# States turned to rows by VectorE blocks and a DRAM scratch instead of TensorE transposes, in a fused graph network and expert kernel

## What is computed

```
h = layernorm(x)
for l in 0, 1, 2:
    m    = h @ weight[l]
    aggr = A^T m                      # A = (adj != 0), per graph
    h    = GRU(aggr, h)               # r, z = sigmoid(...), n = tanh(i_n + r*h_n), h = (1-z)*n + z*h
x = x + h
H = gelu(layernorm(x) @ W1 + b1)      # 128 -> 512
probs = softmax(H @ Wg + bg)          # 8 experts; the best one is taken
x = x + probs[e] * (H @ Wd[e] + bd[e])
```

## Time and profile before

| what | value |
|---|---|
| time, median of 3 runs | 492.29 us (492.11 to 492.55) |
| profiled execution, first to last instruction | 490.1 us |
| around that span (median less span) | 2.2 us |
| mean granted TensorE clock | 0.997 of full speed (2.4 GHz) |
| busy, share of the span | TensorE 98%, VectorE 76%, GpSimd 77%, ScalarE 68% |
| graph network, gate, experts | about 12 to 285 us, to 365 us, to 490 us |

### The profile page before, as it was taken

One profiled execution on the slowest core, in us unless ns is written; L12 is line 12 of the kernel. 1 busy time (PEld: TensorE's weight loads), 2 busy tenths in 40 slices (PEclk: granted clock), 3 DMA queues, 4 the chain that ended last, 5 costly groups with the idle time before them and its releaser, 6 DMA issues.

```text
span 490.1 us, 10428 instructions
## 1 busy us (share of the span) xinstructions
PE 480.0 (98%) x3247; PEld 401.9 (82%) x3247; DVE 370.0 (76%) x1158; ACT 334.7 (68%) x595; POOL 376.1 (77%) x371
## 2 busy tenths in 40 slices
PE   8999999999999999999999999999999999999994
PEld 4788888888888888888888877777769999999994
DVE  4898678789887898888887798878977555655552
ACT  4886996667976768966787698988763554445531
POOL 5389986789988899979778656777777776377576
PEclk9999999999999999999999999999999999999998
DMA  8889000000000000000000000111353342233110
GB/s 217 234 242 289 0 1 0 1 1 1 1 1 2 0 1 2 0 3 0 1 0 1 0 2 18 59 62 57 110 136 100 119 124 86 71 97 90 33 48 24
DMA packets 37317, 27.38 MB, mean 56 GB/s; under 512 B 6140, under 2 KB 33920, under 8 KB 37264
## 3 DMA queue, kind: packets, MB, share of 16 engines
q1 hardware_dynamic: 31344, 17.40, 12.8%
q0 software_dynamic: 4320, 8.93, 5.2%
q10 hardware_dynamic: 1600, 0.40, 0.4%
HBM read 17.12 MB, written 10.04 MB: 55 GB/s over the span
## 4 chain that ended last, share of the span: by engine, by line
PE 94%; ACT 2%; DVE 2%; POOL 1%; issue 1%; POOLq 0%; DVEq 0%
PE bank L484 20%; PE bank L486 19%; PE bank L485 19%; PE bank L736 13%; PE bank L507 4%; PE bank L531 4%; PE bank L530 4%; PE bank L672 3%; PE bank L722 2%; PE bank L629 1%; PE bank L596 1%; PE bank L537 1%; ACT adj_i L948 1%; PE bank L564 1%; PE bank L569 0%
## 5 line engine op out<-in xcount | busy, mean ns | idle before, releaser
L948 ACT ACTIVATE adj_i<-bank,b1c 128x512 f32<-128x512 f32 (+1 forms) x136 | 91.3, 685 | 72.8 <-PE bank L486 72.3
L375 POOL TENSOR_TENSOR diff<-hT,n_sb 128x512 f32<-128x512 f32 x48 | 77.1, 1607 | 12.0 <-ACT n_sb L834 12.0
L451 POOL DMA_INDIRECT sorted_rows<-xrow,pos x64 | 62.2, 972 | 20.0 <-issue 17.9
L736 PE MATMUL bank<-wd_sb,adj_i 128*128 x568 | 66.7, 275 | 0.0
L377 POOL TENSOR_TENSOR diff<-z_sb,diff 128x512 f32<-128x512 f32 x48 | 63.5, 1323 | 3.8
L736 PEld LDWEIGHTS bank<-wd_sb,adj_i 128*128 128x128 f32 x568 | 65.1, 192 | 0.2
L484 PE MATMUL bank<-ag_hi,wf_hi 128*128 128x512 f32 x144 | 61.0, 424 | 0.0
L484 PE MATMUL bank<-hT_hi,w_hi 128*128 128x512 f32 (+1 forms) x136 | 58.3, 429 | 0.9 <-ACT adj_i L948 0.7
L486 PE MATMUL bank<-ag_hi,wf_lo 128*128 128x512 f32 x144 | 57.1, 397 | 0.0
L485 PE MATMUL bank<-ag_lo,wf_hi 128*128 128x512 f32 x144 | 56.7, 394 | 0.0
L484 PE MATMUL bank<-hT_hi,whh_hi 128*128 128x512 f32 x132 | 54.0, 409 | 0.0
(11 more groups left out here) (185 smaller groups left out, 1158.2 us busy)
## 6 DMA issues: line engine op xcount, KB each, us to landing
adj_i<-sorted_rows SPq DMA_DIRECT2D x71, 72.0 KB
xrow<-in_x_dram SPq DMA_DIRECT2D x16, 256.0 KB, 3.7
adj_i<-in_adj_dram SPq DMA_DIRECT2D x16, 256.0 KB, 4.0
sorted_rows<-xrow,pos POOLq DMA_INDIRECT x64, 2.3
sorted_rows<-padrow SPq DMA_DIRECT2D x9, 72.0 KB
out_dram<-cand,home POOLq DMA_INDIRECT x39
bd_bc<-in_L_ffn_bd_dram SPq DMA_DIRECT2D x1, 512.0 KB, 4.1
out_dram<-n_sb,home POOLq DMA_INDIRECT x32
```

The costliest lines, as they stand in the source:

```text
L375: nc.gpsimd.tensor_tensor(diff[:, b, :], hT[:, g, :], n_sb[:, b, :], ALU.subtract).then_inc(diff_ok, 1)
L451: nc.gpsimd.indirect_dma_start(out=sorted_rows, out_offset=bass.IndirectOffsetOnAxis(ap=pos[:, g, j:j + 1], axis=0), in_=xrow[:, g * GR + ...
L736: last = nc.tensor.matmul(o, HT[:, sg % 2, k, j * P:(j + 1) * P], wd_sb[:, bass.ds(at + k * P, P)], start=(k == 0), stop=(k == KC - 1))
L948: nc.scalar.activation(HT[:, hb, k, 0:n], HB[k][:, 0:n], ACT.Gelu, bias=b1c[:, k:k + 1]).then_inc(done, 1)
```

## The change

For states of layers 0 and 1 (32 of the 48 units) the transposes on TensorE go. VectorE transposes the 32x32 blocks of the state into a tile `blocks`; SyncE writes that to a DRAM scratch `swap` with one DMA of 256 KB, waits until it has landed, and reads it back with four DMAs of 64 KB each, which put the blocks in their places; the result `hn` has nodes on partitions with the four graphs interleaved. The sum over neighbours takes plain float32 operands, four products a unit in place of eight, from `xn` in layer 0 and `hn` in layers 1 and 2; `hn_hi`, `hn_lo` and all that makes them are removed on ScalarE, VectorE and GpSimd. The loads of groups 8 to 15 are issued after the first eight states are turned, the weights of the second half after sixteen.

```diff
+    SUB = 32
+    QP = P // SUB
+    swap = nc.dram_tensor("swap", (2, QP, P, P), fp32).ap()
-        A = sb("A", [P, QUAD, NT], f32r)
+        A = sb("A", [P, QUAD, NT])
-        hn_hi, hn_lo = sb("hn_hi", [P, 2, NT], f32r), sb("hn_lo", [P, 2, NT], f32r)
+        blocks = sb("blocks", [P, 2, NT])
+        hn = sb("hn", [P, 2, NT])
+        TURNED = [u for u in range(UN) if layer(u) < LAYERS - 1]
+        FIRST_LOADS = GROUPS // 2
...
# SyncE
+            def state_turned(k):
+                b = k % 2
+                sp.wait_ge(blk_ok, k + 1)
+                hold(sp, hn_in[b], k // 2 * QP * 16)
+                sp.dma_start(swap[b].rearrange("s p e -> p s e"),
+                             blocks[:, b, :].rearrange("p (s e) -> p s e", s=QP)).then_inc(blk_out, 16)
+                sp.wait_ge(blk_out, (k + 1) * 16)
+                if k >= 2:
+                    sp.wait_ge(ag_ps, made("all", TURNED[k - 2] + QUAD))
+                for f in range(QP):
+                    sp.dma_start(hn[:, b, f * P:(f + 1) * P], swap[b, :, f * SUB:(f + 1) * SUB, :]).then_inc(hn_in[b], 16)
+            for g in range(2, FIRST_LOADS):
+                load_group(g)
+            for k in range(2 * QUAD):
+                state_turned(k)
+            for g in range(FIRST_LOADS, GROUPS):
+                load_group(g)
+            for k in range(2 * QUAD, 4 * QUAD):
+                state_turned(k)
...
+            for k in range(4 * QUAD, len(TURNED)):
+                state_turned(k)
# GpSimd
-                if first(s + 1):
-                    first_rows_low(s + 1)
# TensorE
             def neighbours(u):
                 if layer(u) == 0:
                     hold(pe, adj_ok, made("first", u))
...
+                    rows_of = xn[:, u % QUAD, :].rearrange("p (g e) -> p g e", g=GR)
                 else:
-                    hold(pe, hnhi_ok, made("later", u))
-                    hold(pe, hnlo_ok, made("later", u))
+                    k = made("later", u) - 1
+                    pe.wait_ge(hn_in[k % 2], (k // 2 + 1) * QP * 16)
+                    rows_of = hn[:, k % 2, :].rearrange("p (c g) -> p g c", g=GR)
                 for j in range(GR):
...
-                    nc.tensor.matmul(pAG[:, c], hn_hi[:, u % 2, c], A[:, u % QUAD, c], start=True, stop=False)
-                    last = nc.tensor.matmul(pAG[:, c], hn_lo[:, u % 2, c], A[:, u % QUAD, c], start=False, stop=True)
+                    last = nc.tensor.matmul(pAG[:, c], rows_of[:, j], A[:, u % QUAD, c], start=True, stop=True)
...
-                if exists(u):
+                if first(u):
                     unit_turned(u)
# ScalarE: rows_high, the two halves in opening, and hn_hi in step_gnn removed
# VectorE: rows_low_half, rows_low_early, and hn_lo in step_gnn removed
+            def state_blocks(u):
+                k = made("inner", u) - 1
+                dve.wait_ge(h_ok, made("all", u))
+                hold(dve, blk_out, (k - 1) * 16)
+                nc.vector.transpose(blocks[:, k % 2, :].rearrange("p (s e g) -> p g s e", g=GR, s=QP),
+                                    hT[:, u % QUAD, :].rearrange("p (g s e) -> p g s e", g=GR, s=QP)).then_inc(blk_ok, 1)
...
                     state(s - 2)
+                    if layer(s - 2) < LAYERS - 1:
+                        state_blocks(s - 2)
```

More of the change, by code:

```diff
@@ L171, in build @@
             sem(n) for n in ("hh_ps", "r_ps", "z_ps", "in_ps", "ag_ps", "t_ps", "f_ps"))
[L172 to L175, removed]
+        aghi_ok, r_ok, z_ok, n_ok, hthi_ok, h0_ok, h0hi_ok = (
+            sem(n) for n in ("aghi_ok", "r_ok", "z_ok", "n_ok", "hthi_ok", "h0_ok", "h0hi_ok"))
+        aglo_ok, h_ok, h0lo_ok, rhn_ok, cand_ok, x1_ok, adj_ok = (
+            sem(n) for n in ("aglo_ok", "h_ok", "h0lo_ok", "rhn_ok", "cand_ok", "x1_ok", "adj_ok"))
+        blk_ok, blk_out, hn_in = sem("blk_ok"), sem("blk_out"), [sem("hn_in"), sem("hn_in_odd")]
         bn_ok, mv_ok, var_ok, rstd_ok, xn_ok, shift_ok = (
             sem(n) for n in ("bn_ok", "mv_ok", "var_ok", "rstd_ok", "xn_ok", "shift_ok"))
-        xn_half, x0hi_half = sem("xn_half"), sem("x0hi_half")
-        diff_ok, zd_ok, htlo_ok, x0lo_ok, x0lo_first = (
-            sem(n) for n in ("diff_ok", "zd_ok", "htlo_ok", "x0lo_ok", "x0lo_first"))
+        diff_ok, zd_ok, htlo_ok = (sem(n) for n in ("diff_ok", "zd_ok", "htlo_ok"))
         g_bn, g_mv, g_rstd, g_xn, g_t, g_xhi, g_xlo, g_w1, g_h, g_lg, g_lgT = (
@@ L239, in ahead @@
         def ahead(s):
-            return (3, 3, 2, 1, 3) if s < 3 else (9, 8, 5, 2, 2)
-        STATS, SCALE, NORMAL, SPLIT, EDGES = range(5)
+            return (3, 3, 2, 3) if s < 3 else (9, 8, 5, 2)
+        STATS, SCALE, NORMAL, EDGES = range(4)
         EARLY_STATS = GROUPS - QUAD
@@ L295, in _, with load_group @@
             load_adj(1)
-            for g in range(2, GROUPS):
+            def load_group(g):
                 sp.wait_ge(x_in[g % 2], g // 2 * 16)
@@ L365, in _ @@
             nc.gpsimd.memset(xrow[:, :, TOKEN + 1:ROW], 0.0).then_inc(g_tok, 1)
[L367 to L370, removed]
             def old_state(u):
@@ L498, in unit_turned @@
             def unit_turned(u):
[L499 to L504, removed]
+                hold(pe, xn_ok, made("first", u))
                 hold(pe, h0_ok, made("first", u - 1))
                 for j in range(GR):
-                    last = nc.tensor.transpose(pT[:, j * P:(j + 1) * P], src[:, u % QUAD, j * P:(j + 1) * P], ident[:])
+                    last = nc.tensor.transpose(pT[:, j * P:(j + 1) * P], xn[:, u % QUAD, j * P:(j + 1) * P], ident[:])
                 last.then_inc(t_ps, 1)
@@ L824, in opening @@
                 nc.scalar.activation(wT[:, 3:6, :].rearrange("p g e -> p (g e)"), pGH[:, 0:3 * P], ACT.Copy).then_inc(wt_sb, 1)
-                for ready, part, done in ((xn_half, slice(0, NT // 2), x0hi_half), (xn_ok, slice(NT // 2, NT), x0hi_ok)):
-                    act.wait_ge(ready, 1)
-                    nc.scalar.activation(hn_hi[:, 0, part], xn[:, 0, part], ACT.Copy).then_inc(done, 1)
                 act.wait_ge(hh_tr, 1)
@@ L851, in gate_rows @@
                     last.then_inc(g_xn_act, 1)
-            def rows_high(u):
-                hold(act, xn_ok, made("first", u))
-                nc.scalar.activation(hn_hi[:, u % 2, :], xn[:, u % QUAD, :], ACT.Copy).then_inc(x0hi_ok, 1)
             def rows_turned_high(u):
-                hold(act, t_ps, made("all", u))
+                hold(act, t_ps, made("first", u))
                 nc.scalar.activation(hT_hi[:, u % QUAD, :], pT[:], ACT.Copy).then_inc(h0hi_ok, 1)
@@ L889, in first_step @@
                     normalise(u)
-                rows_high(u)
                 rows_turned_high(u)
@@ L918, in step_gnn @@
                     gate_rows((s - GATE_ROWS) // 2, (s - GATE_ROWS) % 2)
[L919 to L924, removed]
+                if first(u):
+                    rows_turned_high(u)
                 if u == UN:
@@ L934, in step_gnn @@
                     state_high(u)
-                if s >= 3 and first(s + ahead(s)[SPLIT]):
-                    rows_high(s + ahead(s)[SPLIT])
                 if s == FFN_WEIGHTS:
@@ L1060, in fused_low @@
                 tt(wf_lo[:, l, :], WF[l][:, 0:3 * P], wf_hi[:, l, :].bitcast(fp32), ALU.subtract).then_inc(wlo_done, 1)
[L1062 to L1068, removed]
             def opening():
@@ L1076, in opening @@
                 normalise(0, 0)
-                normalise(0, 1).then_inc(xn_half, 1)
+                normalise(0, 1)
                 row_moments(1)
@@ L1096, in first_step @@
                     row_stats(2, range(GR))
-                    rows_low_early(1)
                     row_moments(2)
@@ L1105, in first_step @@
                     adjacency(2)
-                    rows_low_early(2)
                     row_moments(3)
@@ L1114, in first_step @@
                     fused_low(2)
-                    rows_low_early(3)
                     first_rows_low(3)
                     state(0)
+                    state_blocks(0)
                     reset(2)
@@ L1151, in residual @@
                     tt(gx, pF[:].rearrange("p (g n) -> p g n", g=GR), gx, ALU.add).then_inc(x1_ok, 1)
[L1153 to L1159, removed]
                 if exists(s):
@@ L1172, in step_gnn @@
                 between(s)
-                if exists(s + 1):
-                    rows_low(s + 1)
+                if first(s + 1):
+                    first_rows_low(s + 1)
                 if s + 1 == UN:
```

15 lines of the change are left out of this document (removed).

## The result

The changed kernel takes 537.15 us (median of 4 runs, 535.14 to 538.49) against 492.27 us: 1.091 times as long, 95% interval 1.0895 to 1.0928. The prediction said slower, 520.5 us, with a range up to 534; the sign was right, the size was not. The profiled execution spans 533.4 us.

The account below looks back on a forecast made before the run. TensorE, busy 98% of the span, was taken as the bound. Span 490.1 - 14.0 for transposes + 42.2 for waits on the DRAM trip = 518.3, plus 2.2 around it, 520.5 us; range 484 to 534, likeliest case 508 to 533.

Parts of the forecast that it names:

- Bound, and saving: TensorE, busy 98% of the span, sets the time; dropping its transposes saves 0.44 us a step, 14.0 us over 32 units.
- Plain float32 products: Neighbours' sum on TensorE: four products as eight records, 0.87 us against 0.84 before, at most 1.5 us in all; taken as 0.
- Stationary operand with a step of four: TensorE's loads of hn at a 16-byte step: 0 taken, upper end 0.9 us a unit, 28 us over 32 units.
- Rival C: Slower: strided stationary operand costs 0.9 us a unit; 512 us, or 535 with reads on few engines; chance 0.10.
- A: The forecast case: hn reads run on few engines, 520.5 us, own range 508 to 533; chance 0.52.
- VectorE: 0.70 us: Each of 32 block transposes on VectorE takes 0.70 us, between 0.69 and 1.2, replacing hn_lo, so its load stays.
- R = 9.0: DRAM round trip: SyncE wakes 0.1, write 2.9, reads' fixed part 1.9, reads' data on four engines 4.1 us.
- Two steps cannot be shorter than 3.0 + R + 0.85: Blocks ready, round trip, neighbours' use; TensorE waits 1.8 and 0.9 us in turn, 10.6 a period, 42.2 us in all.
- No wait other than in steady state: TensorE's waits for hn rows were priced only as 1.8 and 0.9 us in turn, 32 times, none in layer 0.
- SyncE's moved loads: Loads of groups 8 to 15 and six weight loads, issued later by SyncE, delay nothing that is due: cost 0.
- Cover of the other engines: Work removed from ScalarE, VectorE and GpSimd lies beside a TensorE that never pauses: costed at nothing.
- Rival B: Faster, 483.7 us: reads use all engines; GpSimd's 6.3 us row_scale cycle may delay states, adding at most 7; chance 0.24.

Follow-up runs that it names:

- run without trip and with GpSimd spread: Changed kernel without block transposes, write and reads; neighbours read a constant unit-step tile, GpSimd's row_scale three steps ahead instead of eight: 547.29 us, 0.975, graph stretch 252.7.
- plain products alone: Kernel before with only the neighbours' sums as plain float32 products, transposes kept on TensorE, no DRAM: 560.44 us, 0.993, graph stretch 266.4.
- unit step: Changed kernel with hn read as contiguous runs of 128 columns, rows holding features of mixed graphs: 533.03 us, 1.086 against the kernel before.

## Why the prediction was wrong

- **Bound, and saving.** Right. The transposes were worth 13.5 us (predicted 14.0), shown by the run without trip and with GpSimd spread beside the plain products alone, which change nothing.
- **Plain float32 products.** Right: 0.81 us a unit (0.87).
- **Stationary operand with a step of four: "I take 0".** This is the step that failed: a term put at 0 that measured 27.5 us where nothing is waited for, its upper end of 28. My reason, that loads are off the pace when the products are long, forgot that the neighbours' products are not long: each of the eight is 128 columns and 0.10 us, beside a load of 0.19. When the load went to 0.33 the eight went from 0.81 to 1.66 us. Rival C on top of A was priced at 535 us; 537 came. I gave all of C 0.10.
- **VectorE: 0.70 us.** Too low: 1.12 came, near the upper bound of 1.2. The reason was right for contiguous output (0.712 measured); the strided write was not thought of. In the closed loop half of 0.41 us would be 0.2 us a step, 6 to 7 us in all; this is worked out and wasn't run with the reads as they are in the change.
- **R = 9.0.** The mechanism was right, four engines, and the size too high: 8.06, since the write took 2.3 us and not 2.9, and reads came 5.6 us after their first issue, not 6.0. The waits are smaller than the 42.2 us predicted. From 252.7 to 309.7 us of graph stretch, added in this order, the stationary operand makes 27.4 (to 280.1), a trip with reads on sixteen engines, the block transposes and the moved loads with it, 7.8 (to 287.9), and four engines in place of sixteen 21.8. The last two are the waits, 29.6 us. In another order the terms would differ, since a shorter step only uncovers more wait: unit step alone gave back 3.4.
- **"Two steps cannot be shorter than 3.0 + R + 0.85".** Right in form: with the measured terms it gives 13.3 us, and two inner steps of the last three periods take 13.5 on average. What it lacked is that R grows when the step shrinks. The formula also shows what each term was worth in the closed loop, over its sixteen pairs of steps: 1.04 more for the neighbours 16.6 us, 0.35 more for the blocks 5.6, and 0.94 less for R 15.0 the other way. That last one is luck: with R as it measured, my sum would have been 505.5 us, and the miss nearly twice as large. (In the recorded sum 4 x 1.8 + 4 x 0.9 is 10.8 and not 10.6; unrounded waits give 10.5, so nothing rests on it.)
- **No wait other than in steady state.** Missed: the first state costs a wait of 4.6 us. With sixteen engines the same late state costs 1.0, so most of it belongs to four engines too. And the last states of the first two bursts, with loads or weights issued right behind their reads, have trips of 8.8 us, 0.8 more than the usual 8.0 (steps of 7.5 and 7.1 us, where the later two periods end with 6.7 and 6.8). So SyncE's moved loads, costed at 0, are worth some 1 us in this way; that the loads are the cause is not shown, as no run holds them back and changes nothing else.
- **Cover of the other engines.** Right that their relief is worth nothing. Rival B's note on GpSimd was right as well and measured at 5.2 us.

## What to carry to other kernels

Where a term may be worth anything from 0 to 28 us, look first at how full the resource that it loads is already; a load that is already longer than its product cannot hide a doubling. Look at the outermost dimension of both sides of every DMA: here the same bytes cut with 32 outermost on both sides, in place of 4 on one, were worth 21.8 us. A round trip that feeds a loop is priced by closing the loop (ready + trip + use, over the number of steps it spans), and then again with the next DMA standing behind the last.

## What was not expected of the hardware

- A load of a float32 stationary operand of 128 columns takes 0.19 to 0.20 us at a step of 4 or 8 bytes and 0.33 at 16. With the step of 16 the clock made no difference: neighbours took 1.89 us at 1.2 GHz (38.49 to 40.38) as at 2.4; with unit step they took 1.73 (39.27 to 41.00 in that run) and 0.92.
- A float32 block transpose of 128x512 takes 0.71 us when it writes runs of 32 elements and 1.12 when it writes every fourth.
- A write of 256 KB on all sixteen engines took 2.3 us where the reads on four of them were issued 4.2 us before it, 3.0 where 3.6 us before, and 4.8 where 2.4 us before (32.02 and 34.42).
- With four engines in a DMA of 64 KB the queue counts 12 packets fewer than with sixteen (65136 and 66672 packets, 128 such DMAs).
